# A ScalarE copy into tile order ahead of TensorE's mixing products, and a new place for those products in the step

## The chip, the cores and the metric

The kernel runs on one core of one Trainium2 chip. The metric is the device time of one execution in microseconds; a time is the median of several runs. Engines go by the names of the profile: PE is TensorE's matmul side and PEld its weight loads, DVE is VectorE, ACT is ScalarE, POOL is GpSimd, SP issues DMAs.

## The reference

A block with three residual layers on x of 16 sequences, 256 positions, 128 channels, all float32:

```python
x = x + 0.5 * ffn(layernorm(x))
x = x + attn(layernorm(x))
x = x + 0.5 * ffn(layernorm(x))
# ffn: each row goes through one of 8 experts (argmax of a router) and through a shared expert,
#      down(silu(gate @ x) * (up @ x)), hidden width 256; the two results are added
# attn: bound = circular convolution of x with a key (over channels)
#       hologram[t] = sum over s <= t of d**(t-s) * bound[s]
#       x + g * circular correlation of hologram with a second key
```

The kernel computes the attention as a scan along the positions, h[t] = d*h[t-1] + x[t], and then one 128x128 product per row, because both circular operations are linear over the channels and fold into one matrix, `mix`.

## The kernel before

The 4096 rows are 32 tiles of 128 rows, in 8 groups k of 4 tiles. Row 4p+t of a group lies on partition p of tile t, so a group holds two whole sequences. The kernel has the stages: first FFN's front (norm, transpose, router, ranking, scatter of the rows to expert blocks with indirect DMAs on POOL), first FFN's experts (39 blocks of 128 rows), a **middle stage**, the second FFN's experts, and the end. Everything the change touches lies in the middle stage, from about 129 us to 214 us of the span, which for each group adds the first FFN's result, does the attention, and does the front of the second FFN.

Each engine runs its own in-order list, written out by hand as a loop over steps k = -3 or -4 to 7, and semaphores tie the lists together. In step k:

- **DVE** (`middle`, `front`): `scan(k+2)` (L611), the add of the first FFN's result for group k+4 (L599), `choose(k)` (the argmax, L656 to L662, with the attention's statistics of group k+4 in its gaps), the shared expert's `mult` (L631) or `add_shared` (L599) of the step's first part, `add_retrieved(k+2)` (L618, the attention's result into xres), the statistics for the second FFN's norm (L558 to L569), `place_rows(k)`, the DVE work of the second part.
- **POOL** (`middle`): `rstd` of the attention's norm for group k+4 and of the FFN's norm for group k+2 (L346 to L350), then `scatter(k)`, four indirect DMAs (L357).
- **ACT** (`front`): `evac_rows(k)` (L453), `add_self(k+2)` (L446), `norm("f", k+1)` (L438, four ACTIVATEs), `silu_half` of the first part (L462), `norm("a", k+3)` (L438), `silu_half` of the second part.
- **PE** (`front`): the shared expert's first part (L883 or L891), the router's products (L908), the mixing products of group k+2 (L914, which wait for `scan_done`), the second part, the transposes `turn("f", k+1)` (L869), the ranking products, `turn("a", k+3)`.

`turn("a")` writes the transposed rows of a group in position order (column 4p+t), which the scan needs. The mixing products take one tile each, so their stationary operand is every fourth column of `scanned` (`by_row(scanned[:, q, :])[:, :, t]`): neighbouring columns lie four floats, 16 bytes, apart. `scanned` and PSUM bank `tp["a"]` are reused: the scan of group k waits until the products of group k-2 have ended (`mixed`), `turn("a", k+3)` until `add_retrieved(k+2)` has ended (`x2_done`), and the experts start when the scatters of the last group have landed (`sent`) and the shared expert's parts that are due have ended (`half_done`, `mult_done`).

Of the kernel before, what the change touches and what calls it, by code (L numbers as in the profile page):

```python
# [6 lines left out]
ACT = mybir.ActivationFunctionType  # L7
# [5 lines left out]
P = 128  # L13
C = 128
# [7 lines left out]
TPG = 4  # L22
G = NT // TPG
GC = TPG * P
# [36 lines left out]
def build(nc, x_in, gu_in, dn_in, router_in, bind_in, unbind_in, gate_in, decay_in, out):  # L61
# [9 lines left out]
    with ExitStack() as ctx:  # L71
        def sb(name, shape, dt=F32):
            return ctx.enter_context(nc.sbuf_tensor(name, shape, dt))

        def sem(name):
            return ctx.enter_context(nc.semaphore(name))
# [27 lines left out]
        xa = sb("xa", [P, 2 * TPG, C])  # L104
        xnT = sb("xnT", [P, G, GC])
        scanned = sb("scanned", [P, 2, GC])

        st = {k: sb("st_" + k, [P, TPG, 6]) for k in "fa"}
        mv = {k: sb("mv_" + k, [P, NT, 2]) for k in "fa"}
# [53 lines left out]
        tp = {"f": bank[0], "a": bank[1]}  # L163
# [32 lines left out]
        pad_sent = sem("pad_sent")  # L196
        back_in = [sem(f"back_in{k}") for k in range(G)]
        x1_done = sem("x1_done")
        scan_done, mixed = sem("scan_done"), sem("mixed")
        selfed, x2_done = sem("selfed"), sem("x2_done")  # L200
        blk_in = [sem(f"blk_in{b}") for b in range(NBL)]
        blk_out = sem("blk_out")
# [24 lines left out]
        def by_row(ap):  # L227
            return ap.rearrange("p (j t) -> p j t", t=TPG)

        def valid(k):  # L230
            return 0 <= k < G
# [7 lines left out]
        def parts_at(k, i):  # L239

            return SHARED_PARTS[PER_STEP * (k - 1) + i:][:1] if 1 <= k < G else []
# [30 lines left out]
        def wait_pos(eng, s, value):  # L272

            if value > 0:
                eng.wait_ge(s, value)
# [153 lines left out]
        def _(act):  # L429
# [12 lines left out]
            def add_self(k):  # L442

                act.wait_ge(normed["a"], (k + 1) * TPG)
                for i in range(k * TPG, (k + 1) * TPG):
                    last = nc.scalar.activation(xres[:, i, :], xres[:, i, :], ACT.Identity,  # L446
                                                bias=shift["a"][:, i:i + 1], scale=scale_more[:, i:i + 1])
                last.then_inc(selfed, 1)

            def evac_rows(n):  # L450
                act.wait_ge(turned["f"], n + 1)
                wait_pos(act, gu_done, (n - G + 1) * HH)
                nc.scalar.activation(xnT[:, n % G, :], tp["f"][:], ACT.Copy).then_inc(xnT_ready, 1)  # L453

            def shared(f, g, part):
                if part < HH:
                    silu_half(f * G + g, part)
# [6 lines left out]
            def front(f, k):  # L464
                n = f * G + k
                if valid(k):
                    evac_rows(n)
                if f == 1 and valid(k + 2):
                    add_self(k + 2)
                if valid(k + 1):  # L470
                    norm("f", n + 1, k + 1, xn, k + 1)
                for g, part in parts_at(k, 0):
                    shared(f, g, part)
                if f == 1 and valid(k + 3):
                    wait_pos(act, turned["a"], k + 2)
                    norm("a", k + 3, k + 3, xa, (k + 3) % 2)
                for g, part in parts_at(k, 1):
                    shared(f, g, part)
                if k == G - 1:
                    act.wait_ge(pads_at, f + 1)  # L480
                    send_pads(act, range(PADS_SP, E))
# [66 lines left out]
        def _(dve):  # L548
# [58 lines left out]
            def scan(k):  # L607

                dve.wait_ge(turned["a"], k + 1)
                wait_pos(dve, mixed, k - 1)  # L610
                nc.vector.tensor_tensor_scan(scanned[:, k % 2, :], keep[:], tp["a"][:], 0.0, ALU.mult,  # L611
                                             ALU.add).then_inc(scan_done, 1)

# [248 lines left out]
        def _(pe):  # L862
# [9 lines left out]
            def shared(f, g, part):  # L872
                n = f * G + g
                if part < HH:
                    gate_up(n, g, part)
                else:
                    down(n)
# [17 lines left out]
            def front(f, k):  # L895
                n, q = f * G + k, k % 2
# [4 lines left out]
                if valid(k):  # L901
                    if n == 0:
                        pe.wait_ge(router_ready, 16)
                        pe.wait_ge(const_made, N_CONST)
                    pe.wait_ge(xnT_ready, n + 1)
                    wait_pos(pe, route, n * ROUTE_STEPS)
                    for t in range(TPG):
                        last = nc.tensor.matmul(rt[:, t * E:(t + 1) * E], xnT[:, k, t * P:(t + 1) * P], routerT[:],  # L908
                                                start=True, stop=True)
                    last.then_inc(logits, 1)  # L910
                if f == 1 and valid(k + 2):
                    pe.wait_ge(scan_done, k + 3)
                    for t in range(TPG):
                        last = nc.tensor.matmul(tp["a"][:, t * C:(t + 1) * C], by_row(scanned[:, q, :])[:, :, t],  # L914
                                                mix[:], start=True, stop=True)
                    last.then_inc(mixed, 1)
                for g, part in parts_at(k, 1):
                    shared(f, g, part)
                if valid(k + 1):
                    turn("f", n + 1, xn, k + 1, xnT_ready)  # L920
                if valid(k):
# [128 lines left out]
```

## Time and profile before

| | us |
|---|---|
| median of 3 runs | 293.18 |
| lowest, highest | 292.18, 294.78 |
| the profiled execution | 292.21 |
| its span in the trace | 290.5 |
| PE / PEld busy | 257.8 (89%) / 215.9 (74%) |
| DVE, ACT, POOL busy | 189.4 (65%), 160.3 (55%), 179.4 (62%) |
| L914, products with `scanned` (64 instructions) | 17.2 PE, 15.5 PEld |

The shares are averages over stages with different limits. Times in the prediction are microseconds from the start of the span; a row's idle time in brackets is that of its engine just before it, with what ended it.

### The profile page before, as it was taken

The numbers are of one execution on the slowest core, as the hardware profiler recorded it, in microseconds if no ns is written. First come the engines' busy times: TensorE is split into PE (matmuls) and PEld (weight loads), VectorE is DVE, ScalarE is ACT, GpSimd is POOL, SyncE is SP. The second block draws the span as 40 slices with busy tenths as digits, with TensorE's granted clock in tenths as the row PEclk, the third lists the DMA queues.
The fourth block names the chain that finished last, engine by engine and source line by source line (L and its number), as shares of the span: only waits on it lengthen the run. The fifth ranks groups of instructions, "written<-read, shape, count | busy, mean of one in ns | idle before, by whom it ended". The sixth has DMA issues, their size and how long they took to land.

```text
span 290.5 us, 6435 instructions
## 1 busy us (share of the span) xinstructions
PE 257.8 (89%) x1788; PEld 215.9 (74%) x1788; DVE 189.4 (65%) x734; ACT 160.3 (55%) x374; POOL 179.4 (62%) x260
## 2 busy tenths in 40 slices
PE   0889999979999999986699999999779999999980
PEld 0547677558999999845577878676469999999560
DVE  4796664954555555448999999676845556655355
ACT  2744353236777777326498877732157777777210
POOL 6646777713777777723457888767505758887700
PEclk9999999999999999997679999899999999999997
DMA  6871111323333321144000101101423433311078
GB/s 210 314 310 40 55 47 60 109 69 80 101 98 107 98 78 38 38 122 172 0 1 23 35 28 38 49 29 56 124 66 88 107 88 105 92 55 48 27 250 329
DMA packets 24244, 27.51 MB, mean 95 GB/s; under 512 B 4967, under 2 KB 17645, under 8 KB 23952
## 3 DMA queue, kind: packets, MB, share of 16 engines
q1 hardware_dynamic: 17648, 16.06, 18.6%
q0 software_dynamic: 4544, 8.54, 9.0%
q10 hardware_dynamic: 2016, 2.50, 2.4%
q8 instruction: 14, 0.23, 0.3%
q14 instruction: 22, 0.18, 0.2%
HBM read 15.37 MB, written 12.62 MB: 96 GB/s over the span
## 4 chain that ended last, share of the span: by engine, by line
PE 45%; POOL 17%; DVE 14%; issue 12%; DMA 4%; ACT 3%; SPq 1%; DVEq 1%; ACTq 0%; POOLq 0%
PE bank L960 13%; PE bank L883 12%; POOL returned L386 10%; PE bank L891 6%; PE bank L968 6%; POOL dispatched L357 3%; DMA xres<-in_x 3%; PE bank L908 3%; PE bank L914 2%; DVE st_f L558 2%; DVE hs L631 2%; DVE xres L599 2%; POOL token L380 1%; PE bank L869 1%; POOL scale_f L346 1%
## 5 line engine op out<-in xcount | busy, mean ns | idle before, releaser
L386 POOL DMA_INDIRECT returned<-ey,token x78 | 76.6, 982 | 32.9 <-issue 18.0
L960 PE MATMUL bank<-xsT,wgu 128*128 128x128 f32 x624 | 82.9, 276 | 2.5 <-DVE xres L599 1.5
L960 PEld LDWEIGHTS bank<-xsT,wgu 128*128 128x128 f32 x624 | 75.7, 192 | 3.7 <-DVE xres L599 1.8
L357 POOL DMA_INDIRECT dispatched<-xn,slot x64 | 63.5, 993 | 23.7 <-issue 17.7
L883 PE MATMUL bank<-xnT,gu 128*128 128x512 f32 x128 | 65.1, 636 | 4.3 <-DVE hs L631 3.5
L813 DVE COPY ey<-bank 128x128 f32<-128x128 f32 x78 | 22.8, 292 | 45.6 <-PE bank L968 45.5
L489 ACT ACTIVATE wgu<-gu 128x512 f32 x78 | 48.2, 623 | 4.1 <-issue 3.9
L462 ACT ACTIVATE sg<-bank 128x512 f32<-128x512 f32 x32 | 18.9, 591 | 54.5 <-PE bank L883 47.1
L968 PE MATMUL bank<-wdn,eh 128*128 128x128 f32 x312 | 47.5, 276 | 0.5 <-DVE eh L808 0.5
L511 ACT ACTIVATE eg<-bank 128x256 f32<-128x256 f32 x78 | 29.9, 384 | 32.6 <-PE bank L960 32.4
L968 PEld LDWEIGHTS bank<-wdn,eh 128*128 128x128 f32 x312 | 40.9, 192 | 0.9 <-DVE eh L808 0.9
L883 PEld LDWEIGHTS bank<-xnT,gu 128*128 128x128 f32 x128 | 23.1, 200 | 23.9 <-issue 22.7
L891 PEld LDWEIGHTS bank<-dn,hs 128*128 128x128 f32 x256 | 31.2, 197 | 8.7 <-DVE hs L631 7.3
L891 PE MATMUL bank<-dn,hs 128*128 128x128 f32 x256 | 32.8, 283 | 4.0 <-DVE hs L631 4.0
L808 DVE TENSOR_TENSOR eh<-eg,bank 128x256 f32<-128x256 f32 x78 | 32.1, 411 | 4.4 <-ACT eg L511 4.4
L438 ACT ACTIVATE xn<-xres,shift_f,scale_f 128x128 f32<-128x128 f32 x64 | 26.3, 483 | 15.2 <-POOL shift_f L350 15.2
L631 DVE TENSOR_TENSOR hs<-sg,bank 128x512 f32<-128x512 f32 x32 | 21.8, 681 | 12.5 <-ACT sg L462 12.5
L794 DVE COPY wdn<-dn 128x256 f32 x78 | 23.6, 303 | 3.1 <-issue 3.1
L908 PEld LDWEIGHTS bank<-routerT,xnT 128*128 128x128 f32 x128 | 17.5, 203 | 6.7 <-issue 6.4
L914 PE MATMUL bank<-mix,scanned 128*128 128x128 f32 x64 | 17.2, 419 | 3.9 <-DVE scanned L611 3.9
L914 PEld LDWEIGHTS bank<-mix,scanned 128*128 128x128 f32 x64 | 15.5, 327 | 5.0 <-DVE scanned L611 5.0
L869 PEld LDWEIGHTS bank<-ident,xn 128*128 128x128 f32 x64 | 9.5, 166 | 12.4 <-POOL before L413 7.0
(102 smaller groups left out, 292.9 us busy)
## 6 DMA issues: line engine op xcount, KB each, us to landing
xs<-dispatched SPq DMA_DIRECT2D x80, 66.0 KB, 1.8
ey<-returned SPq DMA_DIRECT2D x16, 256.0 KB, 4.3
gu<-in_gu SPq DMA_DIRECT2D x1, 2048.0 KB, 12.6
out<-xres ACTq DMA_DIRECT2D x8, 256.0 KB, 2.9
returned<-ey,token POOLq DMA_INDIRECT x78
xres<-in_x SPq DMA_DIRECT2D x1, 1024.0 KB, 8.1
dn<-in_dn SPq DMA_DIRECT2D x1, 1024.0 KB, 15.1
dispatched<-xn,slot POOLq DMA_INDIRECT x64
```

Of the source, the lines that this page charges most:

```text
L357: nc.gpsimd.indirect_dma_start(dispatched[:, :], bass.IndirectOffsetOnAxis(slot[:, i:i + 1], 0), xn[:, i, :], None, bounds_check=last_row) ...
L386: nc.gpsimd.indirect_dma_start(returned[:, :], bass.IndirectOffsetOnAxis(token[:, b:b + 1], 0), ey[:, b, :], None, bounds_check=last_back, ...
L438: nc.scalar.activation(dst[:, at * TPG + t, 0:C], xres[:, i, :], ACT.Identity, bias=shift[kind][:, i:i + 1], scale=scale[kind][:, i:i + 1] ...
L489: nc.scalar.activation(wgu[:, b % WR, :], tile(gu, expert_of(digits[0], b)), ACT.Copy).then_inc(blk_wgu, 1)
L511: nc.scalar.activation(eg[:, b % WR, :], bank[4 + b % WR][:, 0:H], ACT.Silu).then_inc(blk_silu, 1)
L631: nc.vector.tensor_tensor(hs[:, n % 2, h, :], sg[:, h, :], u_ps[h][:], ALU.mult).then_inc(mult_done, 1)
L808: nc.vector.tensor_tensor(eh[:, b % WR, :], eg[:, b % WR, :], bank[4 + b % WR][:, H:2 * H], ALU.mult).then_inc(blk_mul, 1)
L883: last = nc.tensor.matmul(ps[:], gu[:, SHARED, at:at + P], xnT[:, g, :], start=True, stop=True)
L891: last = nc.tensor.matmul(o_ps[:, t * C:(t + 1) * C], hs[:, n % 2, h, t * P:(t + 1) * P], dn[:, SHARED, h, :], start=(h == 0), stop=(h == ...
L914: last = nc.tensor.matmul(tp["a"][:, t * C:(t + 1) * C], by_row(scanned[:, q, :])[:, :, t], mix[:], start=True, stop=True)
L960: last = nc.tensor.matmul(bank[4 + b % WR][:, i * P:(i + 1) * P], wgu[:, b % WR, i * P:(i + 1) * P], xsT[:, b // 2 % 2, b % 2, :], start=T ...
L968: last = nc.tensor.matmul(y_of(b), eh[:, b % WR, h * P:(h + 1) * P], wdn[:, b % WR, h * C:(h + 1) * C], start=(h == 0), stop=(h == HH - 1))
```

## The change

A second buffer, `by_tile_T`, two slots of 128x512 floats, is added. In each step that has a group k+2, ACT gets one more instruction behind `add_self(k+2)` and ahead of `norm("f", k+1)`: a copy of the 512 scanned values of each partition from position order into tile order. It waits for the scan of that group and for the products of the group two before it (whose slot it writes), and signals `sorted_done`. The products wait for `sorted_done` instead of `scan_done`, take 128 adjoining columns of `by_tile_T` as stationary operand, and stand behind the step's second part instead of ahead of it. The scan of group k waits for the copy of group k-2 instead of for its products.

```diff
+        by_tile_T = sb("by_tile_T", [P, 2, GC])
...
-        scan_done, mixed = sem("scan_done"), sem("mixed")
+        scan_done, sorted_done, mixed = sem("scan_done"), sem("sorted_done"), sem("mixed")
...
+            def sort_scanned(k):
+
+                act.wait_ge(scan_done, k + 1)
+                wait_pos(act, mixed, k - 1)
+                nc.scalar.activation(by_tile_T[:, k % 2, :].rearrange("p (t j) -> p t j", t=TPG),
+                                     scanned[:, k % 2, :].rearrange("p (j t) -> p t j", t=TPG),
+                                     ACT.Copy).then_inc(sorted_done, 1)
...
                 if f == 1 and valid(k + 2):
                     add_self(k + 2)
+                    sort_scanned(k + 2)
                 if valid(k + 1):
                     norm("f", n + 1, k + 1, xn, k + 1)
...
                 dve.wait_ge(turned["a"], k + 1)
-                wait_pos(dve, mixed, k - 1)
+                wait_pos(dve, sorted_done, k - 1)
...
+                for g, part in parts_at(k, 1):
+                    shared(f, g, part)
                 if f == 1 and valid(k + 2):
-                    pe.wait_ge(scan_done, k + 3)
+                    pe.wait_ge(sorted_done, k + 3)
                     for t in range(TPG):
-                        last = nc.tensor.matmul(tp["a"][:, t * C:(t + 1) * C], by_row(scanned[:, q, :])[:, :, t],
+                        last = nc.tensor.matmul(tp["a"][:, t * C:(t + 1) * C], by_tile_T[:, q, t * P:(t + 1) * P],
                                                 mix[:], start=True, stop=True)
                     last.then_inc(mixed, 1)
-                for g, part in parts_at(k, 1):
-                    shared(f, g, part)
```

## Rows read from the trace of the kernel before

**Rows 1.** The chain that ended last: shares of the span by engine.
```profile
PE 45%; POOL 17%; DVE 14%; issue 12%; DMA 4%; ACT 3%; SPq 1%; DVEq 1%; ACTq 0%; POOLq 0%
```

**Rows 2.** Windows: length, busy PE, PEld, DVE, ACT, POOL, granted clock, DMA.
```profile
140.00:146.60 6.60, 4.76 (x19) 3.87 (x19) 6.21 (x28) 3.03 (x8) 3.83 (x8) 0.50 0.00 0
153.70:178.60 24.90, 24.32 (x150) 19.46 (x148) 23.62 (x103) 19.06 (x47) 21.13 (x28) 1.00 0.10 34
180.60:184.00 3.40, 3.40 (x6) 1.23 (x7) 2.19 (x11) 1.77 (x5) 2.72 (x3) 0.51 0.20 63
```

**Rows 3.** Timeline of POOL in the middle stage: start, length, instruction, idle before.
```profile
153.69 1.01 POOL L346 TENSOR_TENSOR scale_f<-var_f,minus_half 128x4 f32<-128x4 f32 x1 [0.75 <-DVE minus_mean_f L569]
155.14 1.45 POOL L357 DMA_INDIRECT dispatched<-xn,slot  x1 [0.17 <-issue]
...
170.10 1.01 POOL L346 TENSOR_TENSOR scale_f<-var_f,minus_half 128x4 f32<-128x4 f32 x1
...
184.22 1.05 POOL L346 TENSOR_TENSOR scale_f<-var_f,minus_half 128x4 f32<-128x4 f32 x1
...
192.18 1.04 POOL L346 TENSOR_TENSOR scale_f<-var_f,minus_half 128x4 f32<-128x4 f32 x1 [1.57 <-DVE minus_mean_f L569]
...
207.77 0.97 POOL L357 DMA_INDIRECT dispatched<-xn,slot  x1 [0.30 <-issue]
```

**Rows 4.** Timeline where the second FFN's experts start.
```profile
210.31 5.27 SPq L313 DMA_DIRECT2D xs<-dispatched  x6
...
213.25 0.39 ACT L505 ACTIVATE xsT<-bank 128x256 f32<-128x256 f32 x1 [0.21 <-PE bank L949]
...
213.85 1.86 PEld L960 LDWEIGHTS bank<-xsT,wgu 128*128 128x128 f32 x16 [0.84 <-DVE xres L599]
```

**Rows 5.** Weight loads: two lines by form (busy, mean ns), two in the timeline.
```profile
L891 PEld LDWEIGHTS bank<-dn,hs 128*128 128x128 f32 x256 | 31.2, 197 | 8.7 <-DVE hs L631 7.3 <-issue 1.4
...
L914 PEld LDWEIGHTS bank<-mix,scanned 128*128 128x128 f32 x64 | 15.5, 327 | 5.0 <-DVE scanned L611 5.0
...
163.01 1.94 PEld L914 LDWEIGHTS bank<-mix,scanned 128*128 128x128 f32 x8
...
164.86 1.88 PEld L891 LDWEIGHTS bank<-dn,hs 128*128 128x128 f32 x16
```

**Rows 6.** Lines by form: an ACT copy, and two DVE reductions of 40 elements.
```profile
L489 ACT ACTIVATE wgu<-gu 128x512 f32 x78 | 48.2, 623 | 4.1 <-issue 3.9
...
L662 DVE TENSOR_REDUCE chosen<-chosen 128x8 bf16<-128x40 bf16 x16 | 3.6, 226 | 0.5
...
L784 DVE TENSOR_REDUCE tab_exp<-packed 128x5 int32<-128x40 f32 x2 | 0.4, 196 | 0.1
```

**Rows 7.** Timeline of the first steps: scan, products and add of the first groups.
```profile
137.32 2.13 PE L914 MATMUL bank<-mix,scanned 128*128 128x128 f32 x8 [1.31 <-DVE scanned L611]
...
139.49 0.69 DVE L618 TENSOR_TENSOR xres<-bank,xres 128x512 f32<-128x512 f32 x1
...
141.68 1.21 DVE L611 TENSOR_TENSOR_SCAN scanned<-keep,bank 128x512 f32<-128x512 f32 x1
...
142.95 2.24 PE L914 MATMUL bank<-mix,scanned 128*128 128x128 f32 x8 [1.60 <-DVE scanned L611]
...
145.23 0.69 DVE L618 TENSOR_TENSOR xres<-bank,xres 128x512 f32<-128x512 f32 x1
...
151.33 0.68 DVE L618 TENSOR_TENSOR xres<-bank,xres 128x512 f32<-128x512 f32 x1
```

**Rows 8.** Timeline of step 2, from its scan to the next.
```profile
161.74 1.22 DVE L611 TENSOR_TENSOR_SCAN scanned<-keep,bank 128x512 f32<-128x512 f32 x1
...
163.63 1.65 ACT L438 ACTIVATE xn<-xres,shift_f,scale_f 128x128 f32<-128x128 f32 x4 [1.44 <-POOL shift_f L350]
...
165.79 0.69 DVE L631 TENSOR_TENSOR hs<-sg,bank 128x512 f32<-128x512 f32 x1
...
169.50 1.21 DVE L611 TENSOR_TENSOR_SCAN scanned<-keep,bank 128x512 f32<-128x512 f32 x1
```

## The prediction

> **What bounds the kernel now.** I read the page's chain first. It gives PE 45% of the span and POOL 17% [rows 1], and a chain over the whole program can't say what one stage is worth, so I went to the stage that the change touches, the middle one, by windows. From 153.7 to 178.6 PE is busy 24.32 of 24.90, DVE 23.62, POOL 21.13, ACT 19.06 [rows 2]. Three engines look full; the timeline tells which one is waited for. POOL begins at 153.69 with the statistics of group 2, after a wait for DVE of 0.75, and from there works off its list with nothing ahead of an instruction but its own issue gaps: 155.14, 170.10 and 184.22 stand for all of them, 28 by 178.6 [rows 2, 3]. At 192.18 it waits for DVE once more, 1.57, for the statistics of the last group; behind that stand 12 scatters, the last of which starts at 207.77 [rows 3]. SP can load the experts' blocks only when these have landed (210.31); ACT ends the first evacuation at 213.25 + 0.39 = 213.64, and PE starts the experts at 213.85, where its own last wait is for a DVE result [rows 4]. So two paths end almost together there: POOL's, and the shared expert's on PE and DVE. The reader is to see that PE's busy share is no bound here: the stage's length is when POOL begins (153.69), POOL's fixed work, and when the last statistics come (192.18).
>
> **What the change takes away.** The load of a stationary operand with columns 16 bytes apart takes 327 ns, with adjoining columns 197; in a row, eight go in 1.94 and sixteen in 1.88 [rows 5], so 0.2425 and 0.1175 each. A group's products have eight: they shrink from 1.94 to 0.94, by 1.0 at full clock, 8.0 for eight groups. At half clock I take twice 0.1175, 0.235, eight in 1.88: nothing is won there, because the strided loads take about the same at both clocks (2.13 at 137.32, 2.24 at 142.95 inside the half-clock stretch [rows 2, 7]).
>
> **What it adds: the copy's length.** No row has a strided ACT copy. Below, it is an adjoining copy of 512 elements, 0.623 [rows 6]. Above, all of it goes at the ratio of the loads, 0.2425/0.1175 = 2.06, so 1.28. Between: the load of these very bytes at this very step pays 327 - 197 = 130 ns for 128 columns, 1.02 ns a column; for 512 that is 0.52, and the copy 1.15. A DVE reduction that reads 40 elements 16 bytes apart (L662) takes 226, one over 40 adjoining ones (L784) 196 [rows 6]: 0.75 an element, 0.38 for 512, a copy of 1.0. I take 1.15, since the load reads the same data at the same step; 0.62 and 1.28 stay for the range.
>
> The row shows TensorE alone paying for the step. The Trainium skill, "Advanced Engine Details and Errata", section "SBUF Cachelines", speaks against the change: lines are 16 bytes, full speed needs two hits on a line, and a new line at each access is penalised, whatever the engine. By that rule the penalty moves to ScalarE and doesn't go away; the two DVE rows agree, and no row of ScalarE shows it. The Trainium skill, "Vector Engine (DVE) Microarchitecture Reference", section "Measured stream behaviour on trn2", has 1.73 against 1.054 ns an element for one hopping source; an estimate from it is 0.62 + 512 x 0.68 ns = 0.97, and the sum would be +1.5 instead of the +2.3 below.
>
> **What waits for the copy.** In ACT's list the copy stands ahead of `norm("f", k+1)`, the first part's silu, `norm("a", k+3)` and the second part's silu; all of these now wait for the scan. On PE the products wait for the copy, and behind them stand both transposes and the ranking. The scan's wait for the copy of two groups before is long met. No DMA is moved or added. The copy's plain occupancy, three in the 24.90 window, takes ACT from 19.06 to 22.5 [rows 2], which fits; the order is what costs.
>
> **The first groups.** Group 0: the scan ends at 137.27, the copy at 138.45, the products at full clock (0.94 and a tail of 0.1) at 139.5; DVE was busy until the add at 139.49 [rows 7]: +0.05. Group 1: the scan at 141.68 ends 142.95, a little late, the copy 144.15. The clock is at 0.50 from 140 to 146.6 [rows 2], so the products take 1.98 and end near 146.2; the add was at 145.23 [rows 7]: +1.0. Group 2: DVE is full up to the add at 151.33 [rows 7], so it keeps +1.0, and POOL, which waited for DVE at 153.69 [rows 3], starts 1.0 late. With a copy of 0.62 the same working gives +0.3, with full clock and 0.62 about 0.
>
> **The steady steps.** Step 2 is the pattern [rows 8]. The scan runs 161.74 to 162.96. ACT had been idle 1.44 when the norm started at 163.63, waiting for POOL: a copy of 0.62 ends at 163.63 and is free. That idle time is its cover. A copy of 1.15 ends at 164.16, and the norm starts 0.5 late. DVE's multiply at 165.79 starts when the norm (1.56 to the next instruction) and a silu of 0.6 are through, so it is 0.5 late too, and with it the add, the statistics and the next scan at 169.50, since DVE has hardly a gap (23.62 of 24.90 [rows 2]). The same working gives +0.3 in step 1 and +0.3 in step 3, where another instruction was the later one by 0.2: DVE is 1.0 + 0.3 + 0.5 + 0.3 = 2.1 late at step 4. For steps 4 and 5 I add 0.2: the products stand behind a part of 1.88 now and win 1.0 themselves, but the longest chain there is again copy, norm, silu, multiply, add. So the last group's add is 2.3 late.
>
> **The sum.** POOL's instruction at 192.18 waited for just that [rows 3], so it is 2.3 late; its 12 scatters, the landing, the first transposes and the evacuation at 213.25 [rows 4] follow at their own pace. The experts start 2.3 late, and nothing behind is changed. The profiled execution took 292.21 for a span of 290.5; 292.21 + 2.3 = 294.5. It stands 0.97 under the median of 293.18; on the median that is 295.5, slower by 0.8%. By the copy's length: 0.62 gives +0.3 at the start and about -0.5 at the end (the half-clock part at 180.6 to 184 [rows 2] no longer stands ahead of group 7's transposes; ACT's list allows no more), so -0.2; the slope is 2.5 over 0.53, 4.7 for each us of copy; 1.28 gives +2.9.
>
> **The rivals.**
> - *PE is the bound after all.* Then all 8.0 come off: 285.2. For it: 45% of the chain, PE busy 24.32 of 24.90. Against it: POOL's row without waits between 153.69 and 184.22, which no faster product shortens. 0.05.
> - *The copy pays nothing for the step.* It is then 0.62, hidden in the 1.44 of ACT idle, and the result is not slower: -0.2, 293.0. For it: nothing but that no row of ACT shows a penalty; against it: two other engines pay. It decides at a copy of about 0.66, where the slope crosses zero. 0.25.
> - *PE's clock falls once more.* The products come after two parts now; if a stretch such as 180.6 to 184 (clock 0.51, 3.40 long [rows 2]) falls on the second part and the products of step 4 or 5, the add waits for both, and half of 3.40 is lost: +2.3 + 1.7 = +4.0, 297.2. For it: PE waits for ACT more than before, and in the half-clock stretch at 140 it was also waiting between its groups, busy 4.76 of 6.60. Against it: the columns in a step stay the same. It decides as soon as the stretch lies between the last three adds. 0.18.
> - *The forecast*: 0.52.
>
> **How the numbers follow.** The likeliest is 295.5. Its own range goes from a copy of 1.0 (+1.6, 294.8) to one of 1.28 and a half-clock third group (+0.5 more, +3.4), 296.6. The range takes in the free copy down to 292.5 and the clock case up to 298.0; left out are the PE case (0.05), the low edge of the free copy (0.06) and the high edge of the clock case (0.06). Runs of one kernel differ by nearly 1%, so 1% is what can be told from no change: above 296.1 lie the clock case (0.18) and the upper three tenths of the forecast (0.16), 0.34; below 290.2 only the PE case, 0.05; 0.61 between.
>
> **What would show it.** The copy's mean in the groups by line (1.15 or 0.62) decides most. Loads of L914's successor: 0.1175 apart at full clock. In the timeline: the add of group 1 near 146.2, POOL's first FFN statistics of group 2 near 154.7, ACT's norm starting right behind the copy and not behind POOL's shift in steps 2 and 3, POOL's wait ahead of the last statistics longer than 1.57, the experts' first load near 216.1 instead of 213.85. The forecast is wrong if ACT's norm still waits for POOL, if the clock from 140 to 146.6 is full, or if DVE has gaps that take up the delay.

## The result and the profile after

The changed kernel took 300.71 us (median of 4 runs, 299.72 to 301.45) beside 292.86 for the kernel before: ratio 1.0255, interval 1.0209 to 1.0301. Two repeats of the same kernel among later experiments gave 297.99 (1.0142, 1.0080 to 1.0204) and 296.66 (1.0129, 1.0026 to 1.0232). It is slower each time, by 1.3 to 2.6%; on the median of 293.18 the repeats stand for 297.3 and 297.0. The forecast was 295.5, its range 292.5 to 298.0: the repeats lie inside it, the first result 2.7 above it.

The groups by line of the profile after (busy, mean ns of one, idle before and what ended it) answer to [rows 5, 6]:

```profile
L901 PEld LDWEIGHTS bank<-dn,hs 128*128 128x128 f32 x256 | 31.6, 199 | 9.7 <-DVE hs L641 8.3 <-issue 1.4
L926 PEld LDWEIGHTS bank<-mix,by_tile_T 128*128 128x128 f32 x64 | 9.1, 217 | 9.5 <-ACT by_tile_T L455 9.0 <-issue 0.5
L455 ACT ACTIVATE by_tile_T<-scanned 128x512 f32<-128x512 f32 x8 | 9.1, 1133 | 7.6 <-DVE scanned L621 7.5
```

The copy takes 1.133; the products' loads fell from 15.5 in all to 9.1, but PE now waits 9 us for copies where it waited 5.0 for scans.

The timeline of the first groups (start, length, instruction, idle before) answers to [rows 7]; its first row is the first add of the experts' results, with which the middle stage begins:

```profile
132.54 0.69 DVE L609 SCALAR_TENSOR_TENSOR xres<-ey,xres 128x512 f32<-128x512 f32 x1 [0.55 <-DMA ey<-returned]
...
139.70 1.21 DVE L621 TENSOR_TENSOR_SCAN scanned<-keep,bank 128x512 f32<-128x512 f32 x1
...
140.94 1.12 ACT L455 ACTIVATE by_tile_T<-scanned 128x512 f32<-128x512 f32 x1 [1.19 <-DVE scanned L621]
...
142.12 1.69 PE L926 MATMUL bank<-mix,by_tile_T 128*128 128x128 f32 x8 [2.52 <-ACT by_tile_T L455]
143.85 0.69 DVE L628 TENSOR_TENSOR xres<-bank,xres 128x512 f32<-128x512 f32 x1 [0.76 <-PE bank L926]
...
150.58 0.69 DVE L628 TENSOR_TENSOR xres<-bank,xres 128x512 f32<-128x512 f32 x1 [1.15 <-PE bank L926]
...
156.69 0.68 DVE L628 TENSOR_TENSOR xres<-bank,xres 128x512 f32<-128x512 f32 x1
```

In the kernel before the same first row starts at 129.16. So 3.4 us of this execution lie ahead of anything that the change touches; neither repeat has them (129.34 and 129.49, below). They arise near the start of the program: DVE waits 1.19 for a load of x at 15.14 (0.23 before), and then the clock is at half, 1.2 GHz, in a stretch where the kernel before has it full (columns as in [rows 2]):

```profile
23.10:26.50 3.40, 3.40 (x5) 1.32 (x6) 0.67 (x2) 0.00 (x0) 2.44 (x3) 0.50 0.12 40
```

Counted from the first back-add, the adds of groups 0, 1 and 2 come at 11.31, 18.04 and 24.15, before at 10.33, 16.07 and 22.17: 1.0, 2.0 and 2.0 late. DVE, which had no gap ahead of these adds, waits for PE's products ahead of two of them.

Windows of the profile after (columns as in [rows 2]), the stretch of those groups and the first products of the second experts:

```profile
142.60:152.80 10.20, 6.66 (x31) 5.59 (x29) 7.96 (x41) 8.16 (x20) 4.31 (x8) 0.50 0.00 0
...
221.10:224.50 3.40, 3.20 (x15) 3.23 (x16) 0.42 (x1) 0.38 (x1) 0.00 (x0) 0.50 0.25 60
```

A steady step, as [rows 8]:

```profile
167.63 1.21 DVE L621 TENSOR_TENSOR_SCAN scanned<-keep,bank 128x512 f32<-128x512 f32 x1
...
168.88 1.15 ACT L455 ACTIVATE by_tile_T<-scanned 128x512 f32<-128x512 f32 x1 [1.24 <-DVE scanned L621]
...
169.93 1.63 ACT L439 ACTIVATE xn<-xres,shift_f,scale_f 128x128 f32<-128x128 f32 x4
...
172.07 0.69 DVE L641 TENSOR_TENSOR hs<-sg,bank 128x512 f32<-128x512 f32 x1 [0.41 <-ACT sg L471]
...
175.82 1.21 DVE L621 TENSOR_TENSOR_SCAN scanned<-keep,bank 128x512 f32<-128x512 f32 x1
```

Scan to scan is 8.19 here and 7.76 before: 0.43 of growth. The norm starts right behind the copy, with no wait for POOL, 2.30 behind the scan's start instead of 1.89.

POOL, as [rows 3], and the start of the second experts, as [rows 4]:

```profile
159.05 1.01 POOL L347 TENSOR_TENSOR scale_f<-var_f,minus_half 128x4 f32<-128x4 f32 x1 [0.75 <-DVE minus_mean_f L579]
...
183.22 1.01 POOL L347 TENSOR_TENSOR scale_f<-var_f,minus_half 128x4 f32<-128x4 f32 x1 [0.32 <-DVE minus_mean_f L579]
...
198.12 1.04 POOL L347 TENSOR_TENSOR scale_f<-var_f,minus_half 128x4 f32<-128x4 f32 x1 [1.78 <-DVE minus_mean_f L579]
...
213.71 0.97 POOL L358 DMA_INDIRECT dispatched<-xn,slot  x1 [0.30 <-issue]
```

```profile
217.76 4.18 SPq L314 DMA_DIRECT2D xs<-dispatched  x5
219.77 0.30 PE L959 MATMUL bank<-ident,xs 128*128 128x128 f32 x1 [2.15 <-DMA xs<-dispatched]
```

POOL's last scatter ends at 214.68, 82.14 behind the first back-add (before 208.74, 79.58): 2.56 later. But SP loads only 3.08 behind that end; before it was 1.57. PE, which went from its last shared part straight into the transposes before, now waits 2.15. The kernel before at that place, with its first 16 expert products at full clock:

```profile
212.32 0.30 PE L949 MATMUL bank<-ident,xs 128*128 128x128 f32 x1
...
213.88 2.02 PE L960 MATMUL bank<-xsT,wgu 128*128 128x128 f32 x16 [0.68 <-DVE xres L599]
```

The table gives these stages for all kernels that ran, each from its one profile, in us: the start of the first back-add (L599 or its successor); from there to the end of POOL's last scatter; from there to SP's first load of rows; from there to the first expert product; and from that to the start of PE's last row. Each later kernel ran beside the kernel before on the same chip (medians of the latter: 293.06 for e1 to e4, 293.05 for e5 to e8, 294.11 for e9 to e12, 294.20 for e13 and e14). Some runs, most of them of the kernel before, take over 1.5% more than the fastest of the same kernel: the medians are over all runs, the ratios leave such runs out, so that e12 has 1.0129 although its medians differ by 0.9%.

| kernel | back-add | middle | landing | to experts | experts | median | ratio |
|---|---|---|---|---|---|---|---|
| before | 129.16 | 79.58 | 1.57 | 3.57 | 67.36 | | |
| changed, first result | 132.54 | 82.14 | 3.08 | 3.54 | 68.51 | 300.71 | 1.0255 |
| changed, again (e1) | 129.34 | 82.29 | 3.40 | 3.36 | 69.65 | 297.99 | 1.0142 |
| buffer alone (e2) | 129.99 | 77.72 | 1.57 | 3.43 | 67.29 | 293.19 | 0.9985 |
| place alone (e3) | 129.32 | 80.20 | 3.71 | 3.61 | 69.61 | 296.64 | 1.0079 |
| copy alone (e4) | 129.35 | 84.05 | 3.71 | 3.48 | 68.46 | 300.63 | 1.0233 |
| changed, 12 products at the start (e5) | 130.95 | 82.65 | 1.66 | 3.91 | 68.64 | 297.46 | 1.0175 |
| before, 52 products at the start (e6) | 146.37 | 78.08 | 1.60 | 4.14 | 67.36 | 311.1 | 1.0618 |
| changed, adjoining copy (e7) | 128.99 | 79.20 | 1.55 | 3.96 | 68.32 | 296.62 | 1.0094 |
| changed, filler in groups 0 to 2 (e8) | 130.41 | 81.81 | 1.84 | 4.03 | 68.33 | 296.44 | 1.0117 |
| changed, 24 ahead of experts (e9) | 130.45 | 82.34 | 2.89 | 3.50 | 68.69 | 298.45 | 1.0156 |
| changed, filler at both (e10) | 130.90 | 81.04 | 1.65 | 3.84 | 67.53 | 296.76 | 1.0123 |
| before, filler in groups 0 to 2 (e11) | 130.65 | 79.33 | 1.65 | 3.53 | 67.28 | 293.55 | 0.9987 |
| changed, third time (e12) | 129.49 | 82.30 | 1.65 | 4.06 | 68.32 | 296.66 | 1.0129 |
| changed, 48 ahead of experts (e13) | 128.94 | 82.63 | 1.57 | 4.95 | 67.04 | 297.25 | 1.0109 |
| before, later landing (e14) | 129.17 | 79.40 | 4.07 | 3.61 | 69.27 | 297.72 | 1.0133 |

### The profile page after: what moved, and what is told of

Same layout as the page of the kernel before. It is cut to its first block, busy times and chain, and to the rows that moved or that the text cites. A ratio compares the mean times of both kernels' runs of the same rounds, so it can differ in the third digit from the quotient of the medians.

```text
span 299.4 us, 6449 instructions
## 1 busy us (share of the span) xinstructions
PE 254.6 (85%) x1788; PEld 211.2 (71%) x1788; DVE 188.6 (63%) x734; ACT 168.4 (56%) x382; POOL 178.6 (60%) x260
## 4 chain that ended last, share of the span: by engine, by line
PE 41%; DVE 16%; POOL 15%; issue 13%; DMA 7%; ACT 4%; SPq 2%; DVEq 1%; ACTq 0%; POOLq 0%
PE bank L970 13%; POOL returned L387 9%; PE bank L893 9%; PE bank L978 6%; PE bank L901 5%; POOL dispatched L358 4%; DMA xres<-in_x 3%; PE bank L918 2%; PE bank L879 2%; DVE st_f L568 2%; DVE hs L641 2%; DVE xres L609 2%; ACT xn L439 2%; DVE xres L628 2%; PE bank L926 2%
## 5 line engine op out<-in xcount | busy, mean ns | idle before, releaser
L970 PE MATMUL bank<-xsT,wgu 128*128 128x128 f32 x624 | 84.2, 279 | 2.4 <-ACT xsT L515 1.7
L970 PEld LDWEIGHTS bank<-xsT,wgu 128*128 128x128 f32 x624 | 77.2, 195 | 3.3 <-ACT xsT L515 1.5
L901 PE MATMUL bank<-dn,hs 128*128 128x128 f32 x256 | 33.5, 286 | 4.9 <-DVE hs L641 4.9
L641 DVE TENSOR_TENSOR hs<-sg,bank 128x512 f32<-128x512 f32 x32 | 21.8, 682 | 15.5 <-ACT sg L471 15.5
L804 DVE COPY wdn<-dn 128x256 f32 x78 | 23.1, 297 | 2.7 <-issue 2.7
L381 POOL TENSOR_TENSOR token<-xs,to_replica 128x2 int32<-128x2 int32 x40 | 8.4, 210 | 18.1 <-PE bank L959 17.6
L879 PE MATMUL bank<-ident,xn 128*128 128x128 f32 x64 | 12.6, 315 | 7.5 <-POOL before L414 7.4
L568 DVE BATCH_NORM_STATS2 st_f<-xres 128x6 f32<-128x128 f32 x64 | 14.2, 281 | 7.1 <-DMA xres<-in_x 6.6
```

The lines of the kernel that those rows point to most:

```text
L641: nc.vector.tensor_tensor(hs[:, n % 2, h, :], sg[:, h, :], u_ps[h][:], ALU.mult).then_inc(mult_done, 1)
L901: last = nc.tensor.matmul(o_ps[:, t * C:(t + 1) * C], hs[:, n % 2, h, t * P:(t + 1) * P], dn[:, SHARED, h, :], start=(h == 0), stop=(h == ...
L970: last = nc.tensor.matmul(bank[4 + b % WR][:, i * P:(i + 1) * P], wgu[:, b % WR, i * P:(i + 1) * P], xsT[:, b // 2 % 2, b % 2, :], start=T ...
```

## The experiments

**The changed kernel again, and a third time.** No edit.

> The changed kernel as it is, beside the others. In its profile the first expert stage already starts some 3.2 us late (65.77 against 62.42 for PE's first transposes there), ahead of every changed instruction. Theory A, input loads and clock of that execution: this part of the delay comes and goes, and the ratio stays between 1.015 and 1.03. Theory B, the added buffer and semaphore change something in the stages before: it is there again, with a ratio of 1.02 to 1.03.

> The changed kernel once more, beside the other runs of this call. First result: ratio 1.0255 with a part of 3.4 us that came ahead of any changed instruction (in the load of x); second: 1.0142 without that part. If the part ahead belongs to the execution and not to the change, the stage before the first back-add is again about 129.3 long, as in the kernel before, and the total 297.5 to 298.5; if it belongs to the change, 300.5 to 301.5 and the first back-add at 132.

1.0142 and 1.0129; the 296.66 of the second lies under the expected 297.5 to 298.5. The third time's first back-add, and its first expert products:

```profile
129.49 0.69 DVE L609 SCALAR_TENSOR_TENSOR xres<-ey,xres 128x512 f32<-128x512 f32 x1 [0.48 <-DMA ey<-returned]
...
217.50 3.07 PE L970 MATMUL bank<-xsT,wgu 128*128 128x128 f32 x16 [0.68 <-ACT xsT L515]
```

The 3.4 us ahead of the middle stage belong to the first profiled execution and not to the change. The middle stage is the same in all three, 82.1 to 82.3. Why all four runs of the first result lie above those of the repeats stays open; only one of the four was profiled.

**The buffer alone.**

```diff
+        by_tile_T = sb("by_tile_T", [P, 2, GC])
+        sorted_done = sem("sorted_done")
```

> The kernel before with the buffer by_tile_T and the semaphore sorted_done added and never used; nothing else differs. Theory A (the early 3.2 us are the state of the loads and of the clock in an execution): the ratio is 1.000, within 0.004. Theory B (addresses in SBUF or numbers of semaphores cost time): the ratio is about 1.01, 295 to 297 us.

0.9985 (0.9955 to 1.0016): the layout costs nothing.

**Each half of the change alone.** The place alone moves the old products behind the second part; the copy alone leaves the new ones ahead of it.

```diff
-                if f == 1 and valid(k + 2):
-                    pe.wait_ge(scan_done, k + 3)
...
                 for g, part in parts_at(k, 1):
                     shared(f, g, part)
+                if f == 1 and valid(k + 2):
+                    pe.wait_ge(scan_done, k + 3)
...
```

> Only the products are moved behind the second part; they still read scanned at every fourth column and wait for the scan. My prediction's theory (the copy's wait on ACT is the cost, the new place is nearly free): within 1 us of before. Rival (the place costs, because the last groups' add waits for a part and for strided loads): 2 to 4 us slower.

> Only the copy and the adjoining columns; the products stay in their old place, ahead of the second part. Copy theory: slower than before by 2 to 3 us plus whatever is common with the run of the whole change, since ACT's norm still waits behind the copy. Rival (the place of the products is the cost): within 1 us of before.

The place alone: 1.0079 (1.0038 to 1.0119), some 2.3 us, over the expected 1 and inside the rival's 2 to 4; its landing takes 3.71 and its experts 69.61. The copy alone: 1.0233 (1.0165 to 1.0302).

Their middle stages, 80.20 and 84.05, are to be read with the clock. Five profiles have the old order and no copy. Three of them have a stretch of 3.4 at half clock near 182, as in [rows 2], and take 79.3 to 79.6 (before, e11, e14); two have none and take 77.7 and 78.1 (e2, e6). The copy alone has such a stretch (183.6 to 187.0) and is 4.5 to 4.7 above the three. The place alone has none and is 2.1 to 2.5 above the two. The whole change has none in any of its three profiles and is 4.1 to 4.6 above the two. So the copy is enough for the delay, in either place. Up to the add of group 5 the copy alone and the whole change (e1) are level, 48.52 and 48.49 behind the first back-add; the 1.8 between them (84.05 and 82.29) arises in groups 6 and 7, where that stretch falls. What the new place is worth beside the copy is not shown.

**A copy without the stride.** It reads and writes adjoining values, so the reordering is left out.

```diff
-    by_tile_T[:, k % 2, :].rearrange("p (t j) -> p t j", t=TPG),
-    scanned[:, k % 2, :].rearrange("p (j t) -> p t j", t=TPG),
+    by_tile_T[:, k % 2, :], scanned[:, k % 2, :],
```

> The changed kernel with the copy reading its 512 values in their own order; the values are not put into tile order, so the attention's rows are mixed up; everything else is the same. My theory of the step in the copy: the copy takes 0.62 instead of 1.13, ACT's norm waits for POOL again in the steady steps, and POOL's last scatter ends 1.5 to 2.5 us earlier than in the changed kernel. Rival (the place in ACT's list costs, whatever the copy's length): under 1 us earlier.

Its group by line:

```profile
L455 ACT ACTIVATE by_tile_T<-scanned 128x512 f32<-128x512 f32 x8 | 5.0, 631 | 8.1 <-DVE scanned L619 8.1
```

Half a microsecond less of copy takes 3.1 off the middle stage (82.29 to 79.20, both without a half-clock stretch near 182), over the expected 1.5 to 2.5: the slope is 3.1/0.50 = 6 us for each us of copy, with 4.7 forecast. The steady steps are those of the kernel before: in step 2 the norm starts 1.89 behind the scan's start, as before (2.30 with the stride). Against e2 and e6 the middle stage is still 1.1 to 1.5 longer, and that comes from the first groups: their products run at half clock, 2.08 each, and the add of group 2 is 1.0 later than in the profile before (23.17 against 22.17 behind the first back-add), where the prediction had 0.3 for a copy of 0.62.

The total is 1.0094 (1.0026 to 1.0161), some 2.8. Its profile, of the shortest of its runs, is 1.4 longer than the one before (291.9 and 290.5), with 68.32 for the experts and a later begin. So something is lost behind the middle stage without the stride too; the rest of the 2.8 is not shown.

**Filler in the first groups.** 16 products of constants ahead of the mixing products of groups 0 to 2, in the changed kernel and in the one before; nothing reads them.

```diff
+                    if k <= 0:
+                        for _ in range(16):
+                            nc.tensor.matmul(bank[7][:, 0:P], ones[:], ones[:], start=True, stop=True)
                     pe.wait_ge(sorted_done, k + 3)
```

> The changed kernel with 16 bfloat16 products of 128 columns in front of PE's wait for the copy in the first three steps, where PE has nothing to do for about 2.7 us each; they write a PSUM bank that is rewritten later. Clock theory (the products of groups 0 and 1 run at half clock, which I had taken at full clock for group 0): the clock stays at full in more of 135 to 155 us, the adds of groups 0 to 2 come 1 to 2 us earlier, and POOL starts its row that much earlier. Rival (the copy alone makes the start late): the adds stay where they were, or come later by what the extra products take.

> The kernel before with 16 products of constants ahead of the mixing products of each of groups 0 to 2; nothing else is changed. Theory (the first groups are paced by their chain of scan, products and add, and PE's clock falls there because PE waits for the scans): granted clock 1.0 over most of 130 to 155, products of groups 0 to 2 of 2.0 as before (the strided loads take the same at both clocks), but the shared parts, transposes and router's products between them shorter; the adds of groups 1 and 2 come 0 to 1 earlier, POOL's statistics of group 2 start 0 to 1 earlier than 153.7, total 0 to 1.5 under the kernel before (291.6 to 293.1). Rival (DVE alone paces these groups): the clock is full and nothing comes earlier, total unchanged within 0.5.

Timeline of the changed kernel with it:

```profile
139.93 1.16 PE L929 MATMUL bank<-mix,by_tile_T 128*128 128x128 f32 x8 [1.57 <-ACT by_tile_T L455]
141.12 0.69 DVE L628 TENSOR_TENSOR xres<-bank,xres 128x512 f32<-128x512 f32 x1 [0.22 <-PE bank L929]
...
146.93 0.69 DVE L628 TENSOR_TENSOR xres<-bank,xres 128x512 f32<-128x512 f32 x1 [0.22 <-PE bank L929]
...
154.56 0.69 DVE L628 TENSOR_TENSOR xres<-bank,xres 128x512 f32<-128x512 f32 x1 [1.13 <-PE bank L929]
```

The products of group 0 take 1.16 instead of 1.69, and the adds of groups 0 and 1 come 10.71 and 16.52 behind the first back-add (repeat e1: 11.65 and 18.37; before: 10.33 and 16.07). At full clock the copy costs these two groups 0.4 in all (0.1 in e10, which has the same filler: 10.32 and 16.13), so most of their delay is the half clock. Group 2's products ran into a half-clock stretch again (1.84) and lost most of the gain, and the total (1.0117, 1.0057 to 1.0177) can't be told from that of the changed kernel. In the kernel before the filler changes nothing (0.9987, 0.9941 to 1.0032): DVE paces its first groups there, whatever the clock.

**The instruction fetch.** The trace has DMA queues of their own for instructions: on q8 14 transfers of 16 KB in each profile of the kernel before and of the changed one, on q14 28 or 29 of 8 KB. In the first profile after one of q8 falls on the last scatter. The DMA part of 214 to 218 in the profile after, and of 211 to 213.5 in the third time's, where none does (packets, MB, share; for an issue the us to its landing):

```profile
q8 instruction: 1, 0.02, 1.6%
...
dispatched<-xn,slot POOLq DMA_INDIRECT x1, 3.8
```

```profile
dispatched<-xn,slot POOLq DMA_INDIRECT x1, 2.4
```

The scatter lands in 3.8 with the fetch and in 2.4 without; by its packets, 30 of 32 are through by 215.6 and two start only when the fetch ends (215.5 to 216.5). The trace does not name a packet's DMA engine; that these two share it with the fetch is inferred from the times. To move the fetch against the work without touching the middle stage, products of one column were put at PE's start: 12 in the changed kernel, 52 in the one before.

```diff
             pe.wait_ge(const_made, 1)
+            for _ in range(12):
+                nc.tensor.matmul(bank[7][:, 0:1], ident[:], ident[:, 0:1], start=True, stop=True)
             steps(first_ffn, 1)
```

> The changed kernel with 12 one-column products of the identity (24 loads and 24 matmuls on PE) ahead of everything, into a PSUM bank that is rewritten later; they move the places in PE's program at which its next 16 KB of instructions are fetched. In the traces so far that fetch falls on the last scatter in every kernel with a changed order, and the last scatter lands 3.1 to 3.7 us after its instruction, against 1.6 in the kernel before. Fetch theory: the fetch comes some 24 matmuls earlier in the program, off the last scatter, and the landing takes 1.6 again; the total is 1.5 to 3 us under the changed kernel. Rival (the landing is late for another reason, such as the pads or the idle SP queue): the landing stays at 3.1 to 3.7.

> The kernel before with 52 such products (104 matmuls) ahead of everything, so that the fetch that stands some 5 us ahead of the last scatter's end comes about 24 matmuls later in the program, near it. Fetch theory: the last scatter lands 3 us or more after its instruction instead of 1.6, PE waits longer ahead of the experts, and the total is 1.5 to 4 us over the kernel before, with no change in the middle stage. Rival: landing 1.6, and the total within 1 us of before but for what the products at the start cost (under 1 us, PE waits for the first loads there).

In the changed kernel the fetches of q8 moved (the first to 23.1, from 28.5 to 34.2 in all profiles without these products) and those of q14 did not, so q8 carries PE's instructions; the landing went from 3.40 to 1.66, as expected. But another one (128.1 to 129.3) fell on the load of the first experts' results, which landed 3.6 behind its issue (2.6 in e1):

```profile
130.95 0.69 DVE L609 SCALAR_TENSOR_TENSOR xres<-ey,xres 128x512 f32<-128x512 f32 x1 [1.36 <-DMA ey<-returned]
```

and the total stayed (1.0175, 1.0125 to 1.0225), where 1.5 to 3 less was expected. In the kernel before the fetch came 1.5 behind the last scatter, no test of the landing; the 52 products (104 in the trace) took 22.35 at the start, where I had counted on less than 1, and the first back-add came 17.2 later, most of the 18.0 by which its 311.1 stands above the kernel before. The repeats settle more: the same kernel, unchanged, landed in 3.08, 3.40 and 1.65, with the fetch at 215.5, 212.5 and 206.5. So where the fetch falls varies between executions; it isn't set by the program alone.

**The clock over the second experts.** Filler ahead of the transposes of the changed kernel: 24 products of constants, the same with the filler of the first groups, and 48.

```diff
                 pe.wait_ge(table_ready, f + 1)
+                if f == 1:
+                    for _ in range(24):
+                        nc.tensor.matmul(bank[7][:, 0:P], ones[:], ones[:], start=True, stop=True)
                 turn_pair(0)
```

> The changed kernel with 24 bf16 products of constants in PE's list between the middle stage and the second experts' first transposes, where PE otherwise waits for the scattered rows; their results are not read. Theory 1 (the expert stage is longer because PE idles 2.2 to 2.8 us there and its clock then falls to half over the first blocks): no row at half clock between 212 and 226, and the stretch from the first expert product to PE's last one is 67.3 to 67.5, as in the kernel before, against 68.5 to 69.7 in the changed kernel; total 1.1 to 2.3 less than the changed kernel of the same call. The last scatter still lands late, 3 to 3.7 us behind its end, because the instruction fetch there is set by what PE has consumed before, not by what stands behind. Theory 2 (the stage is longer because of transfers left over from the late scatter): the clock is full and the stretch stays at 68.5 or more.

> The changed kernel with 16 products of constants ahead of the mixing products of each of groups 0 to 2 and 24 ahead of the second experts. My account of the change is: late add of the groups (copy, half clock in the first groups), late landing (an instruction fetch on it), half clock in the first experts. If it is complete, this kernel keeps only the first term: POOL's last scatter ends 2 to 2.5 after that of the kernel before (counted from the first back-add), lands 1.6 to 1.9 behind its end, the expert stretch is 67.3 to 67.5, and the total is 2 to 3 above the kernel before (295 to 296). Rival: the three terms are not all; then the rows are as said and the total stays 4 or more above the kernel before.

> As the run with 24 products of constants ahead of the second experts, which left 2.1 us between the last of them and the first expert product and the clock at half there, with 48 of them: 3.0 us at full clock, so that they end beside the landing. Theory 1 (the clock falls over the first experts because PE waits ahead of them): no row at half clock between 212 and 226, first 16 expert products in 2.0 instead of 3.1 to 3.8, stretch from the first expert product to PE's last row 67.3 to 67.5, total 1 to 2 under the changed kernel (1.003 to 1.01 of the kernel before). Theory 2 (something else of the late scatter or of the new order slows the first experts): the stretch stays at 68.3 or more.

The timelines with 24, and with 48:

```profile
215.56 1.50 PE L986 MATMUL bank<-ones 128*128 128x128 bf16 x24
...
219.18 3.65 PE L970 MATMUL bank<-xsT,wgu 128*128 128x128 f32 x16 [0.68 <-ACT xsT L515]
```

```profile
214.34 2.84 PE L986 MATMUL bank<-ones 128*128 128x128 bf16 x48
217.02 0.39 PE L959 MATMUL bank<-ident,xs 128*128 128x128 f32 x2
218.09 2.02 PE L970 MATMUL bank<-xsT,wgu 128*128 128x128 f32 x16 [0.68 <-ACT xsT L515]
```

The run with 24 alone missed its expectation: the landing was late, 2.1 us with only two transposes were left behind the filler, and the clock fell all the same (experts 68.69). With both fillers it stayed full (experts 67.53), and with 48 too (67.04). With 48 the gain went back into the wait, since rows that had landed in 1.57 met PE still at its filler: 4.95 to the first product, and a total of 1.0109 (1.0020 to 1.0199) that is not shown to be under the changed kernel's.

With both fillers the total is 1.0123 (1.0084 to 1.0163), some 3.6 above the kernel before: more than the 2 to 3 that the account of three terms expected, less than the rival's 4. It is also no lower than that of the changed kernel beside it (e12, 1.0129). In its profile the terms shrank as the account has it (middle stage 81.04 against 82.30, experts 67.53 against 68.32), but 1.4 more lies ahead of the first back-add, ahead of the filler; the kernel before with filler (e11, 130.65) has as much there. So the fillers show what the half clock costs stage by stage, and no run shows the total falling with it.

The other way round, a late landing in the kernel before, with nothing of the change:

```diff
                 sp.wait_ge(sent, 16 * NT * (f + 1))
+                if f == 1:
+                    sp.dma_start(spare_col[:], decay_in.partition_broadcast(P)).then_inc(late, 16)
+                    sp.wait_ge(late, 16)
```

> The kernel before, with one more load of 128 numbers on SP that must land before SP loads the rows for the second experts; nothing reads what it loads. So the landing alone is late, by the 1.5 to 2.2 of one small transfer, and nothing of the change is in it. Theory 1: PE waits 3 to 4 us instead of 1.5 ahead of the experts, the clock there falls to half over the first of them, and the stretch from the first expert product to PE's last row is 68.3 to 69.7 instead of 67.4; total 2.5 to 4.5 above the kernel before. Theory 2 (a late landing only shifts what is behind it): the clock stays full, stretch 67.4, total 1.5 to 2.2 above the kernel before.

Its timeline, and the window over the first products:

```profile
209.99 0.36 SPq L313 DMA_DIRECT2D spare_col<-in_decay  x1
...
212.64 9.60 SPq L317 DMA_DIRECT2D xs<-dispatched  x10
214.71 0.86 PE L953 MATMUL bank<-ident,xs 128*128 128x128 f32 x2 [2.56 <-DMA xs<-dispatched]
...
216.25 3.75 PE L964 MATMUL bank<-xsT,wgu 128*128 128x128 f32 x16 [0.68 <-ACT xsT L509]
```

```profile
214.70:221.20 6.50, 5.34 (x21) 4.45 (x22) 1.05 (x3) 1.89 (x5) 0.38 (x2) 0.51 0.27 62
```

The load is 2.65 late (209.99 to 212.64) and the first product 2.4 (216.25 against 213.88); then the clock falls to 0.51, 16 products take 3.75 instead of 2.02, and the experts' stretch is 1.9 longer (69.27). By the ratio the kernel is some 3.9 slower (1.0133, 1.0042 to 1.0224), the 2.4 and some 1.5 more. A late landing alone makes the half clock here. The wait is not the whole rule, though: the kernel before with 52 products waited 2.6 there and kept the full clock (67.36), where the changed kernel with the adjoining copy, also at 2.6, lost it (68.32).

## Why the prediction was wrong

**Right.** The copy: 1.15 forecast, 1.11 to 1.18 measured, 0.63 without the stride; ScalarE pays for the step as TensorE does. The Trainium skill, "Advanced Engine Details and Errata", section "SBUF Cachelines", said that a new 16-byte line at each access is penalised; ScalarE's rows agree, with 1133 against 631 ns for 512 values. The free-copy rival thus falls, by its own condition. Loads: eight in 0.97 at full clock, with 0.94 forecast, and in 1.78 at half, with 1.88. The steady steps: +0.43 in step 2 (forecast +0.5), and from group 2 to group 6 the adds' delay grows by 1.4 in the profile after (1.98 to 3.38) and 1.1 in e1, with 1.3 forecast. Right too: copy, norm, silu, multiply as the chain, POOL's wait longer than 1.57 (1.78), and that PE is not the bound.

**Group 0 was mis-sized.** The step said "the products at full clock (0.94 and a tail of 0.1) at 139.5 ...: +0.05". The copy pushes the products from 137.32 to 139.02 (e1), into the half clock: they take 1.44 to 1.93 in the three profiles of the changed kernel, and the scan itself is 0.4 late (e1); the add came 0.7 to 1.3 late. With group 1's own share the delay is 2.0 to 2.5 at group 2, not 1.0, and POOL's statistics of group 2 start 2.0 late (159.05 - 132.54 = 26.51 against 24.53). I had read the clock of 140 to 146.6 [rows 2] as fixed in time, and took the products of group 0 to lie just ahead of it. In the changed kernel PE waits longer between these groups (2.52 ahead of the products instead of 1.31), and the stretch at half clock is 10.2 long. Its length alone is no sign of the change: with the layout alone (e2) it is 17.1, from 137.9 to 155.0, and makes nothing late there (group 2's add 21.34 behind the first back-add, 22.17 before): the strided products take 2.23 in it and 2.13 at full clock. It is the products with adjoining columns that need the full clock: 1.16, and 2.08 at half.

**A gain was left out of the sum, and the middle stage came out near by luck.** Before, the clock is 0.51 from 180.6 to 184 [rows 2], and from group 6's add to group 7's it is 8.96; after, that stretch is gone, the two adds are 8.15 apart, and the delay falls from 3.4 to 2.6. Other runs agree: the three kernels besides before with a half-clock stretch there (e4, e11, e14) have 8.6 to 9.1, those without (e2, e3, e6, e7) 7.3 to 7.7. I had credited 0.5 for it, but only in the case of the free copy. The two errors cancel: POOL's last scatter ends 2.6 to 2.7 late, with 2.3 forecast. That holds against the one profile that I worked from; against e2 and e6, the old order without that stretch, it is 4.1 to 4.6.

**"The landing ... follow at their own pace", "nothing behind is changed".** This is the step that failed in the total. The landing varied from 1.65 to 3.40, with the instruction fetch in the way or not. The fetch meets the last scatter in the first profile, e1, e3, e4 and e9, and in none of the others. That it is the change that draws the two together is not shown: the third time they were apart. The Trainium skill, "Runtime: NRT & Kernel Launch", section "Instruction fetch mechanics", has crossing a 16 KB boundary as mostly hidden. No run here tells whether PE itself waits for a fetch; a data transfer did, by 1.4 (3.8 against 2.4).

And the experts ran longer: 68.3 to 69.7 instead of 67.4, since PE waits ahead of them and its clock falls to half. The kernel before went there with 1.55 us between its last shared part and the first expert product and kept the full clock; the changed one has 2.8 to 3.8. It has more even when the scatter lands on time (third time: 2.77), because PE's last part now ends 2.9 behind POOL's last scatter instead of 3.6, and the second block of rows came 0.5 later behind SP's first load (216.50 - 213.44 = 3.06 against 212.88 - 210.31 = 2.57). I had noted that "two paths end almost together there", and did not ask what PE does while the one comes later than the other.

**The sum, by e12** (span 295.6 against 290.5): 0.33 ahead, 2.72 middle stage, 0.08 landing, 0.49 to the first product, 0.96 experts, 0.52 the end: 5.1. In e1 the landing is 1.83 and the experts 2.29. In the first profile (299.4) it is 3.38 ahead, 2.56, 1.51, 0.0, 1.15 and 0.4; the 3.38 stood in no term of the forecast and is not the change's. Of the rivals, "the clock falls once more" had the right mechanism, at the wrong place: not between the last adds but over the first experts (between the last adds it fell in the copy alone, e4, for 1.8). That its +4.0 is near the repeats' 3.8 and 4.2 is luck: its terms were 2.3 and 1.7, both in the middle stage.

## What to carry to other kernels

A copy that tidies another engine's access pays the same step itself, and its latency stands in every chain that passes it; a busy share that "fits" says nothing of that. Where a stage starts just as PE becomes free, a delay of what it waits for is paid more than once: the wait, and then the products at half clock (2.65 became 3.9 by the ratio of e14). And a stretch of low clock read in one profile is not fixed: near 182 three of five profiles of the old order have it and two do not, with 1.2 to 1.9 between them in the middle stage. Cost an edit at both levels, and compare profiles that have the same stretches.

## What was not expected of the hardware

- During an instruction fetch of 16 KB, one transfer of 0.9 to 1.8 us, two of a scatter's 32 packets were held and with them the landing, 3.8 instead of 2.4; its time against the work differed by 6 us between executions of one program.
- A group's products with stationary columns 16 bytes apart take 2.13 at full and 2.24 at half clock [rows 7]; with adjoining ones 1.16 (e8) and 2.08 (e7, group 0). At half clock tidy columns gain almost nothing, as forecast; unexpected was how many groups they met there.
- A float32 product of one column is not cheap: 52 of them, 104 in the trace, took 22.35 at the start of the program, 0.43 each. That is 0.21 for each of the 104, about what one load of 128 columns takes at half clock (1.78/8 = 0.22). The record has the granted clock at 1.00 there, but the shared expert's four products soon behind them take 3.76 too, and 1.96 later on.
